# Attention and 2:4-sparse FFN in one kernel: low halves of the FFN weights and of the kept activations moved from GpSimd to VectorE

## The chip, the cores and the metric

One core of a Trainium2 chip runs the whole kernel. The metric is the device time of one launch in microseconds (us), the median of several executions.

## The reference

The input x is 2048 tokens by 512. The result is x plus an attention branch plus a feed-forward branch, both fed by the layer-normalised x:

```python
xn = layernorm(x)
# attention: its own layer norm with gamma, beta; residual is xn
h = layernorm(xn) * gamma + beta
q, k, v = h @ Wq, h @ Wk, h @ Wv
a = softmax(causal(q @ k.T / sqrt(512))) @ v @ Wo + xn
# FFN, 512 -> 2048 -> 512: of each 4 neighbouring hidden values the 2 largest by magnitude stay
g = silu(xn @ Wgate) * (xn @ Wup)
f = keep_top2_of_4(g) @ Wdown
out = x + a + f
```

## The kernel before

Everything is float32. A matrix product is made of three products in the format fp32r: each operand is split into a high half (a rounded copy, made by ScalarE) and a low half (operand minus high half, made by VectorE or GpSimd), and TensorE adds high*high, high*low and low*high. So each product needs one copy and one subtraction per operand ahead of it.

**Three stages.** The preamble (to some 50 us) folds the attention weights. The attention stage (to 387 us) goes over 16 query tiles of 128 tokens. The FFN stage (from 387 us) goes over 16 blocks (`N_Q`); block n makes gate and up by a seven-product block scheme (X_hi, X_lo against `wset`), and ends with the down product of block n - 2 (`down`, L735 to L737).

**The attention stage is driven by one hand-written list, `steps`.** Every engine walks the same list and does its own part of each step, in that order, so a wait in one step holds all later steps of that engine. In tile i the list has: `head i` (turn the first two groups of probabilities, PE; copy them to `pT_hi`, ACT L762; subtract to `pT_lo`, DVE L944), `scores i+1` (PE; DVE L1063 to L1075 takes them out of PSUM and finds the row maximum), the steps of `beside[i]`, and `attend i` (PE L533 to L535; from group 2 on, the turn, copy and subtraction of a group come here; ScalarE's exponentials of tile i + 1 too; DVE L1086 and L1099 write the rows). `between[i]` stands between `head i` and `scores i+1`, `before[i]` ahead of `head i`. PE may write the scores of tile i + 1 before it attends tile i. A group is up to four key tiles; `pT_hi` and `pT_lo` have two slots.

**Chunks.** The 2048 tokens are four chunks of 512. For each chunk c the list also has `stat` and `x_stats` (means and variances, DVE L992, L996), `x_rstd` (GpSimd L493 to L499), `x_scale` (DVE L1002 to L1009), `row_turn` (PE L565, DVE L1037), `row_store` and `row_spread` (ACT-issued DMAs that bring the row statistics back over 128 partitions, L829), `xt_load`, `xh_pre` (DVE L1022, L1024), `xh` (ACT L794, L798 and DVE L1040), `xn` (DVE L1029, L1031), `xn_store` (ACT-issued DMA L837), and the products `z` and `v` (PE, ACT L807, DVE L1049).

**Weight units.** The FFN weights are split during the attention stage, in 40 units: 32 of gate/up (0 to 31) and 8 of down (32 to 39). Unit u is loaded by SP (256 KB, L389; 512 KB for a down unit, L387), GpSimd makes the four sums of the block scheme in it (L508 to L513, gate/up units only), ScalarE makes the high half (L815, L812), GpSimd the low half (L521, L518), and SP stores both halves to DRAM (L400, L401, L396, L397). FFN blocks load them back (`load_set`, L410). The function `paced` strews `unit` steps over the list in proportion to the PE products between the two `RUN` marks of a run. At step `unit n` of a run with lag l: SP stores unit n-l-1 and loads unit n+1, GpSimd makes the sums of n and the low half of n-l, ScalarE makes the high half of n-l. Run 0 has units 0 to 19 (tiles 0 to 7, lag 2, five buffers), run 1 units 20 to 25 (tiles 7 and 8), run 2 units 26 to 39 (tiles 11 to 14, four buffers at 128 to 160 KB). `load_set(0)` waits until all units are stored.

**FFN block n on DVE:** `first_beats` (of block n-2), `add_sum` x2, `last_beats`, `hidden`, `count_beats`, `keep` 0 and 1, `add_sum` x2, `keep` 2 and 3 (all L1152), `hidden` (L1111), the product L1186, `last_block`, `add_down` x4 (L1121). GpSimd makes the four low halves `hs_lo` of the kept activations of block n-2 (L526), for all but the last two blocks, where DVE does it (`kept_lo`, L1210). PE's `down` waits for them by `hs_ready`.

Of the kernel before, what the change touches and what calls it, by code (L numbers as in the profile page):

```python
# [11 lines left out]
P = 128  # L12
# [14 lines left out]
def attention_ffn(nc, x, x_t, qkv_t, o_proj, gamma, beta, w_units, w_down, out):  # L27
# [27 lines left out]
    def fills(kind, n):  # L55
# [22 lines left out]
               7: [("RUN", 0, 1), ("RUN", 1, 0)],  # L78
               11: [*z[3], *v[3], ("RUN", 2, 0)]}
    beside = {0: [xh_pre[1][0], exp[1], v[0][3], xh_pre[1][1]],  # L80
              1: [exp[2], *xh[1]],
              2: [exp[3], x_scale[2], row_turn[2], row_store[2]],
              3: [v[1][2], exp[4], *stat[3], x_stats[3], x_rstd[3], *xn[1], xt_load[2], xn_store[1], row_spread[2]],
# [4 lines left out]
              8: [xn_store[2], v[2][0], v[2][1], ("RUN", 1, 1)],  # L88
              9: [row_spread[3], xt_load[3], v[2][2], *xh_pre[3]],
              10: [v[2][3], *xh[3], *xn[3], xn_store[3]],  # L90
              NT - 2: [("RUN", 2, 1)]}
# [19 lines left out]
    last_chunk = [(24, 28), (56, 60), (88, 92), (120, 124)]  # L111
# [4 lines left out]
    for r, (first, last, _, places) in enumerate(RUNS):  # L116
# [14 lines left out]
    def paced(some, r):  # L131

        first, last, lag, _ = RUNS[r]
# [36 lines left out]
    with ExitStack() as ctx:  # L170
# [33 lines left out]
        def stages(name, part, shape, dt):  # L204
            return [[at(f"{name}{r}_{i}", place[part] * KB, shape, dt) for i, place in enumerate(run[3])] for r, run in enumerate(RUNS)]

        u_hi, u_lo, u_raw = stages("u_hi", 0, [P, NOP, P], F32R), stages("u_lo", 1, [P, NOP, P], F32R), stages("u_raw", 1, [P, NOP, P], F32)
        d_hi, d_lo, d_raw = stages("d_hi", 0, [P, 2, D], F32R), stages("d_lo", 1, [P, 2, D], F32R), stages("d_raw", 1, [P, 2, D], F32)
# [78 lines left out]
        last_hs_ready = sem("last_hs_ready")  # L287
# [71 lines left out]
        def _(sp):  # L359
# [19 lines left out]
            def load_unit(u):  # L379
                s = slot_of[u]  # L380
                if u == RUNS[2][0]:
# [89 lines left out]
        def _(pool):  # L471
# [16 lines left out]
            for kind, n, k in steps:  # L488
# [15 lines left out]
                elif kind == "unit":  # L504
# [9 lines left out]
                    u = n - RUNS[k][2]  # L514
                    if in_run(u, k):
                        pool.wait_ge(unit_hi, u + 1)
                        if is_down(u):
                            nc.gpsimd.tensor_tensor(stage_of(d_lo, u)[:], stage_of(d_raw, u)[:], stage_of(d_hi, u)[:].bitcast(F32),  # L518
                                                    ALU.subtract).then_inc(unit_lo, 1)
                        else:  # L520
                            nc.gpsimd.tensor_tensor(stage_of(u_lo, u)[:], stage_of(u_raw, u)[:], stage_of(u_hi, u)[:].bitcast(F32),  # L521
                                                    ALU.subtract).then_inc(unit_lo, 1)
# [758 lines left out]
```

## Time and profile before

| what | value |
|---|---|
| median of 3 executions | 889.5 us (888.72 to 890.56) |
| the profiled execution's own time | 888.59 us |
| its span, first to last instruction | 886.8 us |
| busy: PE / PE weight load / DVE / ACT / POOL | 820.0 / 668.4 / 549.7 / 308.6 / 255.6 us |
| mean granted TensorE clock | 0.973 of full speed |
| DMA traffic | 167.40 MB, mean 189 GB/s |

PE is TensorE, PEld its weight load, DVE VectorE, ACT ScalarE, POOL GpSimd, SP SyncE. A line number such as L521 is the line of the kernel before. In a timeline the brackets at the end of a row give the idle time of that engine ahead of the instruction and what released it. Names with q (ACTq, SPq) are the instruction queues that issue DMAs. The span has three parts: preamble to about 50 us, attention to 387 us, FFN to the end.

### The profile page before, as it was taken

The numbers are of one execution on the slowest core, as the hardware profiler recorded it, in microseconds if no ns is written. First come the engines' busy times: TensorE is split into PE (matmuls) and PEld (weight loads), VectorE is DVE, ScalarE is ACT, GpSimd is POOL, SyncE is SP. The second block draws the span as 40 slices with busy tenths as digits, with TensorE's granted clock in tenths as the row PEclk, the third lists the DMA queues.
The fourth block names the chain that finished last, engine by engine and source line by source line (L and its number), as shares of the span: only waits on it lengthen the run. The fifth ranks groups of instructions, "written<-read, shape, count | busy, mean of one in ns | idle before, by whom it ended". The sixth has DMA issues, their size and how long they took to land. (4 is left out here: it accounts for less than half of the span.)

```text
span 886.8 us, 9758 instructions
## 1 busy us (share of the span) xinstructions
PE 820.0 (92%) x3635; PEld 668.4 (75%) x3635; DVE 549.7 (62%) x879; ACT 308.6 (35%) x504; POOL 255.6 (29%) x259
## 2 busy tenths in 40 slices
PE   7987963996969999989999999999999999999997
PEld 5775852885758888878788888887788888888875
DVE  6985475352542333373766766779776677768686
ACT  5425325322132334253432423244343324233341
POOL 3154878783000764000022202220220222022110
PEclk9998996998979999999999999999999999999999
DMA  9544797856210589839544336336418633451202
GB/s 323 175 155 154 257 336 263 294 206 239 90 60 12 200 295 368 320 118 406 239 166 166 122 139 248 154 106 275 173 70 295 246 143 119 166 209 53 95 1 95
DMA packets 49600, 167.40 MB, mean 189 GB/s; under 512 B 5088, under 2 KB 5136, under 8 KB 47120
## 3 DMA queue, kind: packets, MB, share of 16 engines
q1 hardware_dynamic: 38912, 144.46, 43.4%
q10 hardware_dynamic: 10640, 22.31, 7.2%
q8 instruction: 29, 0.48, 0.2%
q14 instruction: 19, 0.16, 0.0%
HBM read 116.40 MB, written 50.36 MB: 188 GB/s over the span
## 5 line engine op out<-in xcount | busy, mean ns | idle before, releaser
L657 PE MATMUL bank<-X_hi,wset 128*128 128x512 f32 x448 | 174.7, 390 | 4.9 <-DVE X_lo L958 2.8
L659 PE MATMUL bank<-X_hi,wset 128*128 128x512 f32 x448 | 174.5, 389 | 0.0
L658 PE MATMUL bank<-X_lo,wset 128*128 128x512 f32 x448 | 174.4, 389 | 0.0
L526 POOL TENSOR_TENSOR hs_lo<-hid_a,hs_hi 128x512 fp32r<-128x512 f32 x28 | 41.6, 1517 | 235.4 <-ACT hs_hi L877 235.4
L657 PEld LDWEIGHTS bank<-X_hi,wset 128*128 128x128 f32 x448 | 84.1, 188 | 23.9 <-issue 6.5
L659 PEld LDWEIGHTS bank<-X_hi,wset 128*128 128x128 f32 x448 | 84.1, 188 | 17.5
L658 PEld LDWEIGHTS bank<-X_lo,wset 128*128 128x128 f32 x448 | 84.1, 188 | 17.3
L735 PE MATMUL bank<-dw,hs_hi 128*128 128x512 f32 x224 | 89.2, 398 | 2.2 <-DVE acc L1121 1.2
L526 POOL TENSOR_TENSOR hs_lo<-hid_b,hs_hi 128x512 fp32r<-128x512 f32 x28 | 41.6, 1517 | 170.5 <-ACT hs_hi L877 170.5
L736 PE MATMUL bank<-dw,hs_hi 128*128 128x512 f32 x224 | 87.4, 390 | 0.0
L737 PE MATMUL bank<-dw,hs_lo 128*128 128x512 f32 x224 | 87.4, 390 | 0.0
L1121 DVE TENSOR_TENSOR acc<-bank,acc 128x512 f32<-128x512 f32 x64 | 43.4, 688 | 57.4 <-PE bank L737 57.0
L533 PE MATMUL bank<-v_hi,pT_hi 128*128 128x512 f32 x136 | 58.6, 431 | 16.2 <-DVE pT_lo L944 16.2
L521 POOL TENSOR_TENSOR u_lo<-u_raw,u_hi 128x896 fp32r<-128x896 f32 x32 | 68.0, 2129 | 13.0 <-ACT u_hi L815 13.0
L533 PE MATMUL bank<-xT_hi,zg_hi 128*128 128x512 f32 (+3 forms) x160 | 59.4, 371 | 0.5 <-DVE zg_lo L1049 0.5
L535 PE MATMUL bank<-xT_hi,zg_lo 128*128 128x512 f32 (+3 forms) x160 | 58.3, 365 | 0.0
L534 PE MATMUL bank<-xT_lo,zg_hi 128*128 128x512 f32 (+3 forms) x160 | 58.2, 364 | 0.0
L534 PE MATMUL bank<-v_lo,pT_hi 128*128 128x512 f32 x136 | 56.3, 414 | 0.0
L535 PE MATMUL bank<-v_hi,pT_lo 128*128 128x512 f32 x136 | 56.2, 413 | 0.0
L735 PEld LDWEIGHTS bank<-dw,hs_hi 128*128 128x128 f32 x224 | 42.0, 188 | 18.7 <-DVE acc L1121 7.8
L868 ACT COPY g_sum<-bank 128x512 f32<-128x512 f32 x48 | 27.9, 581 | 68.9 <-PE bank L659 68.9
L815 ACT CAST u_hi<-u_raw 128x896 fp32r<-128x896 f32 x32 | 29.9, 942 | 57.8 <-POOL u_raw L513 52.6
(161 smaller groups left out, 1554.5 us busy)
## 6 DMA issues: line engine op xcount, KB each, us to landing
wset<-w_operands SPq DMA_DIRECT2D x64, 896.0 KB, 8.0
w_operands<-u_hi SPq DMA_DIRECT2D x32, 448.0 KB, 2.5
w_operands<-u_lo SPq DMA_DIRECT2D x32, 448.0 KB, 3.6
dw<-down_operands SPq DMA_DIRECT2D x14, 1024.0 KB, 6.8
u_raw<-w_units SPq DMA_DIRECT2D x32, 256.0 KB, 4.0
xn_t<-xt_raw ACTq DMA_DIRECT2D x8, 512.0 KB, 4.8
d_raw<-L_ffn_w_down SPq DMA_DIRECT2D x8, 512.0 KB, 6.2
down_operands<-d_hi SPq DMA_DIRECT2D x8, 512.0 KB, 5.7
```

What stands on the lines that cost most here:

```text
L521: nc.gpsimd.tensor_tensor(stage_of(u_lo, u)[:], stage_of(u_raw, u)[:], stage_of(u_hi, u)[:].bitcast(F32), ALU.subtract).then_inc(unit_lo, 1)
L526: nc.gpsimd.tensor_tensor(hs_lo_at(d)[r][:], unit_of(down_half[d], r)[:], hs_hi_at(d)[:, r, :].bitcast(F32), ALU.subtract).then_inc(hs_rea ...
L533: pe.matmul(dst, l_hi, r_hi, start=(n == 0 and flags.get("first", True)), stop=False)
L534: pe.matmul(dst, l_hi, r_lo, start=False, stop=False)
L535: last = pe.matmul(dst, l_lo, r_hi, start=False, stop=(n == len(pairs) - 1 and flags.get("last", True)))
L657: pe.matmul(dst[:], u[:, 0, :], x_hi, start=(first and kt == 0), stop=False, skip_group_check=True)
L658: pe.matmul(dst[:], u[:, 0, :], x_lo, start=False, stop=False, skip_group_check=True)
L659: last = pe.matmul(dst[:], u[:, 1, :], x_hi, start=False, stop=(kt == 1), skip_group_check=True)
L735: pe.matmul(dst, s_hi, d_h, start=(r == 0), stop=False)
L736: pe.matmul(dst, s_hi, d_l, start=False, stop=False)
L737: last = pe.matmul(dst, s_lo, d_h, start=False, stop=(r == G - 1))
L1121: nc.vector.tensor_tensor(acc[:, tile, :], down_bank(i, t)[:], acc[:, tile, :], ALU.add).then_inc(added, 1)
```

## The change

- Low halves of the weight units: from POOL (L518, L521) to DVE, as a step of its own, `unit_lo n`, which makes the low half of unit n-1. `paced` now deals out `unit n` and `unit_lo n` in turn.
- ScalarE makes the high half of unit n-1 at `unit n`, SP stores unit n-2 and loads unit n+1 there.
- Two runs in place of three: units 0 to 21 over tiles 0 to 8, units 22 to 39 over tiles 11 to 14; four buffers in both, the one at 180 KB is dropped, and with it DVE's wait in `scores` of tile 8 until it was stored.
- The statistics of the fourth chunk (`stat[3]`, `x_stats[3]`, `x_rstd[3]`) go from tile 3 to tile 1, behind `xh[1]`.
- `row_spread[3]` and `xt_load[3]` are no longer steps of ScalarE in tile 9; SP issues the same DMAs once all units of run 0 are stored (at `unit_lo 23`, in tile 8).
- The low halves of the kept activations of all blocks: from POOL to DVE, two of them ahead of `hidden(n, 2, ...)` and two behind it.

```diff
-    RUNS = ((0, 20, 2, [*last_chunk, (180, 188)]), (20, 26, 1, last_chunk), (26, NU, 1, [(128, 132), (136, 140), (144, 148), (152, 156)]))
-    RINGS = 5
+    RUNS = ((0, 22, (24, 56, 88, 120)), (22, NU, (128, 136, 144, 152)))
+    RINGS = 4
...
-        total, count = sum(passes(step) for step in some), last + lag + 1 - first
+        total, count = sum(passes(step) for step in some), 2 * (last + 2 - first)
...
-                placed.append(("unit", first + done, r))
+                placed.append(("unit_lo" if done % 2 else "unit", first + done // 2, r))
...
+                elif kind == "unit_lo" and n == RUNS[k][1] + 1:
+                    if k == 0:
+                        for s in range(RINGS):
+                            sp.wait_ge(unit_stored[s], 32 * uses_after[k][s])
...
-                    u = n - RUNS[k][2]
-                    if in_run(u, k):
-                        pool.wait_ge(unit_hi, u + 1)
...
-            for d in range(ND - 2):
-                for r in range(G):
-                    pool.wait_ge(hs_hi_ready, G * d + r + 1)
-                    nc.gpsimd.tensor_tensor(hs_lo_at(d)[r][:], unit_of(down_half[d], r)[:], hs_hi_at(d)[:, r, :].bitcast(F32),
-                                            ALU.subtract).then_inc(hs_ready, 1)
...
+                elif kind == "unit_lo" and in_run(n - 1, k):
+                    u = n - 1
+                    hi, lo, raws = (d_hi, d_lo, d_raw) if is_down(u) else (u_hi, u_lo, u_raw)
+                    dve.wait_ge(unit_hi, u + 1)
+                    nc.vector.tensor_tensor(stage_of(lo, u)[:], stage_of(raws, u)[:], stage_of(hi, u)[:].bitcast(F32),
+                                            ALU.subtract).then_inc(unit_lo, 1)
...
                     keep(i, 2)
                     keep(i, 3)
+                    kept_lo(i, 0)
+                    kept_lo(i, 1)
                 hidden(n, 2, 2, g_sum[2], b_tile(n, 1))
+                if picks:
+                    kept_lo(i, 2)
+                    kept_lo(i, 3)
```

The list after the change, where the steps below speak of it (U is `unit`, L is `unit_lo`, AT `attend`, HD `head`, SC `scores`): tile 1 is HD1 SC2 L1 exp2 xh1 stat3 AT1; tile 2 is HD2 SC3 U2 L2 exp3 x_scale2 row_turn2 AT2 U3; tile 5 is HD5 SC6 L11 U12 exp6 xh2 x_scale3 row_turn3 AT5; tile 8 is HD8 SC9 L21 U22 L22 xn_store2 v2.0 U23 v2.1 L23 AT8; tile 12 is HD12 SC13 L27 U28 L28 U29 L29 U30 AT12 L30 U31 L31 U32 L32; tile 13 is HD13 SC14 U33 L33 U34 L34 U35 L35 AT13 U36 L36 U37 L37 U38 L38; tile 14 is HD14 SC15 U39 L39 U40 L40 U41 L41 AT14. Before, tile 12 had SC13 U31 U32 AT12 U33 U34.

## Rows read from the trace of the kernel before

**Rows 1.** The page, part 1: busy time, share of the span and instructions of each engine

```profile
PE 820.0 (92%) x3635; PEld 668.4 (75%) x3635; DVE 549.7 (62%) x879; ACT 308.6 (35%) x504; POOL 255.6 (29%) x259
```

**Rows 2.** Timeline of PE, attention stage (start, duration; in brackets idle time and releaser)

```profile
76.39 0.37 PE L565 MATMUL bank<-ident,row_stat 128*16 128x128 f32 x1 [5.84 <-DVE row_stat L1009]
...
119.74 0.77 PE L533 MATMUL bank<-v_hi,pT_hi 128*128 128x512 f32 x1 [4.46 <-DVE pT_lo L944]
...
147.12 0.37 PE L565 MATMUL bank<-ident,row_stat 128*16 128x128 f32 x1 [15.24 <-DVE row_stat L1009]
...
209.14 0.45 PE L575 MATMUL bank<-ident,raw 128*128 128x128 f32 x1 [6.95 <-issue]
...
261.32 0.79 PE L533 MATMUL bank<-v_hi,pT_hi 128*128 128x512 f32 x1 [7.44 <-DVE pT_lo L944]
```

**Rows 3.** Windows: us; PE, PEld, DVE, ACT, POOL busy; clock, DMA share, GB/s

```profile
209.10:212.50 3.40, 3.36 (x10) 2.78 (x11) 0.54 (x1) 0.00 (x0) 0.00 (x0) 0.60 0.77 306
...
261.30:266.70 5.40, 5.38 (x18) 4.41 (x18) 1.17 (x2) 1.22 (x3) 0.00 (x0) 0.52 0.33 101
```

**Rows 4.** Groups of instructions by line: low halves on POOL and on DVE

```profile
L521 POOL TENSOR_TENSOR u_lo<-u_raw,u_hi 128x896 fp32r<-128x896 f32 x32 | 68.0, 2129 | 13.0 <-ACT u_hi L815 13.0
...
L958 DVE TENSOR_TENSOR X_lo<-X_raw,X_hi 128x1024 fp32r<-128x1024 f32 x14 | 16.2, 1219 | 0.1
```

**Rows 5.** Timeline of DVE, tiles 3 to 5

```profile
106.32 2.46 DVE L992 BATCH_NORM_STATS2 stats<-xw 128x6 f32<-128x512 f32 x4
...
109.11 3.11 DVE L1029 TENSOR_TENSOR xt_raw<-xt_raw,spread 128x1024 f32<-128x1024 f32 x1
...
115.05 1.37 DVE L1031 TENSOR_TENSOR xt_raw<-xt_raw,spread 128x1024 f32<-128x1024 f32 x1
...
126.37 1.23 DVE L1022 TENSOR_TENSOR xh_raw<-xt_raw,spread 128x1024 f32<-128x1024 f32 x1 [4.20 <-DMA spread<-row_stats]
...
142.89 2.34 DVE L1040 TENSOR_TENSOR xT_lo<-xh_raw,xT_hi 128x512 fp32r<-128x512 f32 x1 [0.56 <-ACT xT_hi L798]
```

**Rows 6.** Timeline of ACT and its queue, tiles 3 to 8

```profile
116.92 0.49 ACTq L829 DMA_DIRECT2D spread<-row_stats  x1
...
132.87 0.94 ACT L815 CAST u_hi<-u_raw 128x896 fp32r<-128x896 f32 x1 [6.79 <-POOL u_raw L513]
...
207.73 0.59 ACT L807 CAST v_hi<-bank 128x512 fp32r<-128x512 f32 x1 [3.63 <-DMA xn_t<-xt_raw]
```

**Rows 7.** Timelines of SP, POOL, DVE and PE, tiles 11 and 12

```profile
298.40 0.64 SPq L389 DMA_DIRECT2D u_raw<-w_units  x1
...
302.24 0.46 POOL L508 TENSOR_TENSOR u_raw<-u_raw 128x128 f32<-128x128 f32 x1 [0.73 <-DMA u_raw<-w_units]
...
318.40 0.15 DVE L1075 TENSOR_SCALAR neg_max<-row_max 128x1 f32<-128x1 f32 x1
...
321.21 0.69 DVE L944 TENSOR_TENSOR pT_lo<-bank,pT_hi 128x512 fp32r<-128x512 f32 x1 [2.67 <-ACT pT_hi L762]
...
323.21 0.39 PE L533 MATMUL bank<-v_hi,pT_hi 128*128 128x512 f32 x1
```

**Rows 8.** Set 0 on SP, a window (columns as rows 3), PE's start

```profile
361.64 2.03 SPq L410 DMA_DIRECT2D wset<-w_operands  x4
...
364.00:372.00 8.00, 7.94 (x40) 6.42 (x38) 2.39 (x4) 2.83 (x4) 0.00 (x0) 1.00 1.02 419
...
387.29 0.47 PE L657 MATMUL bank<-X_hi,wset 128*128 128x512 f32 x1 [2.75 <-DVE X_lo L958]
```

**Rows 9.** FFN: DVE in a block, hidden(2), a window (as rows 3), PE near the end

```profile
688.13 3.43 DVE L1152 SCALAR_TENSOR_TENSOR hid_a<-beats_b,hid_a 128x512 f32<-128x512 bf16 x2
...
L1111 DVE TENSOR_TENSOR hid_b<-g_sum,hid_b 128x512 f32<-128x512 f32 x16 | 25.7, 1605 | 17.3 <-ACT g_sum L904 17.1
...
600.00:640.00 40.00, 37.55 (x159) 29.02 (x158) 36.13 (x47) 17.40 (x26) 5.93 (x4) 1.00 0.54 215
...
856.12 0.47 PE L735 MATMUL bank<-dw_last,last_hi 128*128 128x512 f32 x1 [1.47 <-DVE last_lo L1210]
```

More of the change, by code:

```diff
@@ L106, in key_tiles @@
         return [range(g, min(g + TC, i + 1)) for g in range(0, i + 1, TC)]
-    last_chunk = [(24, 28), (56, 60), (88, 92), (120, 124)]
-    RUNS = ((0, 20, 2, [*last_chunk, (180, 188)]), (20, 26, 1, last_chunk), (26, NU, 1, [(128, 132), (136, 140), (144, 148), (152, 156)]))
-    RINGS = 5
+    RUNS = ((0, 22, (24, 56, 88, 120)), (22, NU, (128, 136, 144, 152)))
+    RINGS = 4
     run_of, slot_of, use_of, uses = {}, {}, {}, [0] * RINGS
     uses_after = []
-    for r, (first, last, _, places) in enumerate(RUNS):
+    for r, (first, last, places) in enumerate(RUNS):
         for u in range(first, last):
@@ L131, in paced @@
     def paced(some, r):
-        first, last, lag, _ = RUNS[r]
-        total, count = sum(passes(step) for step in some), last + lag + 1 - first
+        first, last, _ = RUNS[r]
+        total, count = sum(passes(step) for step in some), 2 * (last + 2 - first)
         placed, gone, done = [], 0, 0
@@ L202, in attention_ffn, with stages @@
         spread[2] = spread[1]
[L204 to L208, printed above, removed]
+        def stages(name, inside, shape, dt):
+            return [[at(f"{name}{r}_{i}", (place + inside) * KB, shape, dt) for i, place in enumerate(run[2])] for r, run in enumerate(RUNS)]
+        u_hi, u_lo, u_raw = stages("u_hi", 0, [P, NOP, P], F32R), stages("u_lo", 4, [P, NOP, P], F32R), stages("u_raw", 4, [P, NOP, P], F32)
+        d_hi, d_lo, d_raw = stages("d_hi", 0, [P, 2, D], F32R), stages("d_lo", 4, [P, 2, D], F32R), stages("d_raw", 4, [P, 2, D], F32)
         X_hi = [at(f"X_hi{o}", 8 * o * KB, [P, 2, W], F32R) for o in range(NOP)]
@@ L380, in load_unit @@
                 s = slot_of[u]
[L381 removed]
+                if u == RUNS[1][0]:
                     sp.wait_ge(prod_full, prod_no["z", NCH - 1, KT - 1] + 1)
@@ L418, in _ @@
                 if kind == "unit":
-                    first, last, lag, _ = RUNS[k]
-                    if n == first:
+                    if n == RUNS[k][0]:
                         load_unit(n)
-                    if in_run(n - lag - 1, k):
-                        store_unit(n - lag - 1)
+                    if in_run(n - 2, k):
+                        store_unit(n - 2)
                     if in_run(n + 1, k):
                         load_unit(n + 1)
+                elif kind == "unit_lo" and n == RUNS[k][1] + 1:
+                    if k == 0:
+                        for s in range(RINGS):
+                            sp.wait_ge(unit_stored[s], 32 * uses_after[k][s])
+                        sp.wait_ge(row_stat_stored, 16 * (NCH - 1))
+                        sp.dma_start(spread[NCH - 1][:], row_stats_dram[NCH - 1].rearrange("v t p -> v (t p)").partition_broadcast(P)
+                                     ).then_inc(spread_loaded, 16)
+                        for h in range(2):
+                            sp.dma_start(xt_raw[NCH - 1][h][:], xt_chunks[NCH - 1][:, 2 * h:2 * h + 2, :]).then_inc(xt_loaded[NCH - 1], 16)
             for s in range(RINGS):
@@ L807, in _ @@
                     nc.scalar.copy(dst[:, k, :], prod_bank[no % PROD_RING][:]).then_inc(prod_hi, 1)
-                elif kind == "unit" and in_run(n - RUNS[k][2], k):
-                    u = n - RUNS[k][2]
+                elif kind == "unit" and in_run(n - 1, k):
+                    u = n - 1
                     if is_down(u):
@@ L825, in _ @@
                         act.wait_ge(xn_ready, 2 * n)
-                    if n == NCH - 1:
-                        for s in range(RINGS):
-                            act.wait_ge(unit_stored[s], 32 * uses_after[1][s])
                     act.dma_start(spread[n][:], row_stats_dram[n].rearrange("v t p -> v (t p)").partition_broadcast(P)).then_inc(spread_loaded, 16)
```

35 lines of the change are left out of this document (12 added, 23 removed).

## The prediction

> **What bounds the kernel now.** I read the page's busy shares first: PE works 820.0 of 886.8 us, POOL only 255.6 [rows 1]. So a change on DVE and POOL can only win or lose in the 67 us in which PE stands still, and in the half-speed clock behind such waits. The timeline of PE says where: five long waits of the attention stage, 5.84, 4.46, 15.24, 6.95 and 7.44 us [rows 2], end on work of DVE or ACT. A wait costs more than itself: behind the fourth the granted clock is 0.60 over 3.4 us and behind the fifth 0.52 over 5.4 us [rows 3], so part of that stretch runs at 1.2 instead of 2.4 GHz, which costs 1.4 and 2.6 us more. From 280 us to the end of attention PE waits for almost nothing, and in the FFN it waits only 2.45 us in the window at 600 us and a little near the end [rows 9].
>
> **What is moved, priced.** A unit's low half took POOL 2.13 us for 896 elements [rows 4]. On DVE the nearest row is 1.22 us for 1024 [rows 4], with 0.69 for 512 [rows 7]: between them, 1.09 us. Forty of them add 32 x 1.09 + 8 x 1.22 = 44.6 us to DVE; 56 kept low halves add 56 x 0.69 = 38.6 us. What counts is where they stand in DVE's order.
>
> **A. Tile 2, loss 3.9 us.** PE waits 5.84 us for x_scale2, which DVE reaches right behind xh1, AT1, HD2 and SC3. The change puts the statistics of chunk 3 into this chain (106.32 to 109.11, 2.8 us [rows 5]) and L2 directly before x_scale2 (1.09). Nothing covers them: +3.9. L1 is free, since DVE waits there for ScalarE's first xT_hi. The sums of that time are done long before L2.
>
> **B. Tiles 3 to 5, gain 8.7 us.** The 15.24 us wait ends a chain on DVE, ACT and DMA that starts behind v1.2: statistics, xn1 to 116.42, the row_spread issued at 116.92 which lets DVE go on at 126.37 [rows 5, 6], xh_pre2, AT4, HD5, SC6, ScalarE's xh2, x_scale3. Off it: the statistics (2.8); xn1 takes 7.3 us and would take 4 x 1.22 = 4.9 without POOL's low halves in its way, I take 5.2, so 2.1; on it L7, 1.09. The DMA, 9.45 us from issue to use, begins 3.85 sooner, and I take another 0.9 off because fewer units are in flight (between 0 and 3). Behind it ACT no longer stands 6.79 us for POOL's sums [rows 6], of which I let 1.9 reach the chain (DVE's part of HD5 and the exponentials; between 0 and 6.8); the low half of 2.34 us that met POOL [rows 5] shrinks by 1.6, and of the 1.9 us between its end (145.23) and PE's restart at 147.12 [rows 2] I take 0.5. L9 and L10 lie in DVE's 4.20 us of waiting for the DMA, L11 beside ScalarE. Sum 8.7. The 4.46 us wait goes too but adds nothing: PE would only wait longer at the same place later. If none of the POOL terms were real the gain is 2.8 - 1.1 = 1.7; the most is 12.
>
> **C. Tile 8, gain 7.5 us.** PE's 6.95 us are for v2.0, whose high half ACT makes at 207.73 after 3.63 us of waiting for the xn store [rows 6]; ACT issues that store behind the high halves of six units, each held by POOL. Now only U22, with unit 21, stands ahead of it in tile 8. Unit 21's buffer holds unit 17, made behind SC8. PE stops at 202.19 (209.14 - 6.95); between SC8 and that lie 78 matmuls of 0.236 us (37.55 us for 159 [rows 9]), so SC8 ends at 183.8. DVE's end of it and L18 give 185.7; store, load, sums, copy are 3.84 (a store taken like the load [rows 7]), 3.84, 2.0 and 0.94: 196.3; the xn store with its issue 4.5 and the two halves of v2.0 1.3: 202.1, when PE stops today. Idle 6.95 plus clock 1.4 minus 0.8 left is 7.5. The DMAs of chunk 3, moved to SP, go out when unit 21 is stored, about 205 us, and are wanted only behind SC10 in tile 9: free; if they came late, the wait at 261.32 would grow by what DVE waits. If units run one period late, all 7.5 are lost.
>
> **D. Tile 12, loss 7.5 us.** PE is full here, and before the change nobody in this tile hung on DVE. Now the load of unit 29 is issued at U28 after unit 26 is stored, hence after L27, and L27 comes after SC13, which DVE ends at 318.55 [rows 7]. Then: L27 to 319.6, two stores and the load issued by 320.7, 3.84 from issue to sums (298.40 to 302.24 [rows 7]), sums 2.0, ScalarE's copy 0.94 at U30. Behind it only may ScalarE copy the third group of tile 12 (0.59), and DVE subtract (0.69): 328.8. Today PE begins that group at 323.21 [rows 7]. So 5.5 us idle, and between 1.4 and 2.6 us of clock [rows 3]: I take 7.5. Bounds: 0, if load and sums hide in less than they did; 12, if the load takes twice as long.
>
> **E. Tiles 13 and 14, loss 1 us (0 to 4).** The same chain, with down units: 512 KB to load instead of 256, but no sums, and each tile is 2 us longer on PE. L33 to L35 take 3.7 us (3 x 1.22) in front of DVE's third group, where it idles 2.67 today [rows 7]: 1.0 over.
>
> **F. Set 0, loss 2 us (0 to 5).** The last unit is now made behind SC15, so set 0 goes out some 8 us later than 361.64 [rows 8] and meets the X loads, which ACT issues in head 15. At 419 GB/s [rows 8] set 0 (3.67 MB) takes 8.8 us and X (2.1 MB) 5.0; some 12 us of both after 370 end at 384, with DVE's sums of X still to come, so 2 us of delay on top of today's 2.75 us wait [rows 8].
>
> **G. FFN, gain 3.7 us.** In a block DVE's keep 2 and 3 took 3.43 us with POOL at work [rows 9]; two of 0.69 us at a spacing of 0.6 take 1.29. hidden(2) takes 1.60 there instead of 0.69 [rows 9]. So 2.1 + 0.9 us are freed against 4 low halves at 0.6; two of these lie in DVE's wait for ScalarE's silu: DVE comes out of a block 0.6 to 1.8 us earlier. PE's full blocks don't wait anyway; the 2.45 us at 600 us [rows 9] hang on DVE, and so do the 1.47 us at 856.12 [rows 9]: 2.4 + 1.3. Bounds: 0 and 4.5. DVE's busiest stretch is 36.13 of 40 us [rows 9] and loses work, so no new bound.
>
> **A rule.** The two keeps stretched to 3.43 us [rows 9] stand beside POOL's low halves. The Trainium skill, SBUF — State Buffer, "shared port pair", says DVE with two SBUF inputs and GpSimd take an exclusive lock for the whole instruction. That speaks against part of this change: the sums stay on POOL, and every new low half on DVE has two SBUF inputs, so each could wait one sum. By it E would be up to 1.5 us larger and G as it is.
>
> **Sum.** +3.9 - 8.7 - 7.5 + 7.5 + 1 + 2 - 3.7 = -5.5 us. The profiled execution, 888.59 us (span 886.8), becomes 883.1; the median of the runs is 0.9 above it, so 884.0.
>
> **Rivals.**
> - *No tile 12 stall* (D and E hide, because units run ahead): 884.0 - 8.5 = 875.5. For it: before, ScalarE made its copies there without waiting much. Against: L27 is tied to SC13 by the list. 0.20.
> - *Slower: the DVE-gated load.* The chain of D holds PE in tiles 13 and 14 as well, each at 7.5: 884.0 + 15 - 1 = 898.0. It decides from a load of about 6 us instead of 3.84, which the 419 GB/s of late attention make possible. For it: DVE is freed in bursts, behind SC and AT, and stores and loads then go out together. Against: down units need no sums, which gives back 2 us. 0.15.
> - *Tile 8 keeps its wait* (unit 21 late): 891.5. Against: fewer units per tile. 0.15.
> - *The FFN gives nothing*: 884.0 + 3.7 = 887.7, within the band. For it: PE's waits there are few. 0.10.
> - Forecast: 0.40.
>
> **How the numbers follow.** 0.2% is 1.8 us, about what a measurement of this kernel can tell from no change. Forecast and first rival are faster (0.60); half of the third rival and the second are slower, with the upper edge of the forecast's own unknowns: 0.25; the rest, 0.15, is within. The forecast's own range is 878 to 890; the range reaches to the first rival and nearly to the second: 874 to 896.
>
> **What would show it.** After: the wait at L565 in tile 2 near 9.7 us; the second one near 11 to 14 and ending near 142 us; no long wait in tile 8; a new one near 5.5 us in tile 12 at the third group, with ACT held by POOL's sums; set 0 issued about 10 us behind SC15; keep 2 and 3 at 1.3 us. Wrong if tile 12 shows no wait, if tile 8 keeps one, or if DVE stands for u_hi in tiles 4 to 8.

## The result, and the profile after

| | before | after |
|---|---|---|
| median of 17 executions each, side by side | 889.5 us (887.3 to 891.9) | 892.8 us (890.4 to 898.8) |
| ratio, 95% interval | | 1.0046 [1.0029, 1.0063] |
| span of the profiled execution | 886.8 us | 897.0 us |
| its own time | 888.59 us | 898.84 us |

The change makes the kernel 0.46% slower; forecast were 884.0 us and a gain. The measured 892.8 us lies inside the range of 874 to 896. The profiled execution of after is the slowest of its 17, 6.1 us above their median, so positions in it are some us late; where that matters I compare with other kernels that run the same code there.

Part 1 of the page of the kernel after, the row that answers to [rows 1]:

```profile
PE 823.1 (92%) x3635; PEld 675.6 (75%) x3635; DVE 574.0 (64%) x975; ACT 308.5 (34%) x504; POOL 88.1 (10%) x163
```

POOL has lost 167.5 us of work and DVE gained only 24.3, although 40 + 56 instructions moved to it. Two things hide in that. The groups of the kernel after (busy, mean ns of one, idle before) show low halves cheaper on DVE than on POOL [rows 4], and the work that POOL used to stretch [rows 9] back at its own length:

```profile
L1041 DVE TENSOR_TENSOR u_lo<-u_raw,u_hi 128x896 fp32r<-128x896 f32 x32 | 35.2, 1119 | 2.0 <-ACT u_hi L804 1.9
...
L1146 DVE TENSOR_TENSOR hs_lo<-hid_a,hs_hi 128x512 fp32r<-128x512 f32 x28 | 18.0, 686 | 0.0
...
L1101 DVE TENSOR_TENSOR hid_b<-g_sum,hid_b 128x512 f32<-128x512 f32 x16 | 11.1, 692 | 0.4
...
L1142 DVE SCALAR_TENSOR_TENSOR hid_a<-beats_b,hid_a 128x512 f32<-128x512 bf16 x16 | 10.4, 684 | 0.0
```

Shares of busy time say nothing more. The timeline of PE of the kernel after does (start, duration, in brackets idle time and releaser); it answers to [rows 2] and the last row of [rows 8]:

```profile
80.71 0.37 PE L556 MATMUL bank<-ident,row_stat 128*16 128x128 f32 x1 [9.56 <-DVE row_stat L995]
...
146.93 0.37 PE L556 MATMUL bank<-ident,row_stat 128*16 128x128 f32 x1 [18.46 <-DVE row_stat L995]
...
180.05 0.79 PE L524 MATMUL bank<-xT_hi,zg_hi 128*128 128x512 f32 x1 [3.94 <-DVE zg_lo L1035]
...
209.35 0.30 PE L566 MATMUL bank<-ident,raw 128*128 128x128 f32 x1 [1.01 <-issue]
...
260.27 0.80 PE L524 MATMUL bank<-v_hi,pT_hi 128*128 128x512 f32 x1 [7.43 <-DVE pT_lo L930]
...
327.13 0.80 PE L524 MATMUL bank<-v_hi,pT_hi 128*128 128x512 f32 x1 [5.51 <-DVE pT_lo L930]
...
353.34 0.80 PE L524 MATMUL bank<-v_hi,pT_hi 128*128 128x512 f32 x1 [2.83 <-DVE pT_lo L930]
...
404.81 0.77 PE L648 MATMUL bank<-X_hi,wset 128*128 128x512 f32 x1 [7.05 <-DVE X_lo L944]
...
880.78 0.47 PE L724 MATMUL bank<-dw_last,last_hi 128*128 128x512 f32 x1 [2.72 <-DVE last_lo L1146]
```

Against before, the tile 2 wait grew from 5.84 to 9.56, the two waits of tiles 3 to 5 (4.46 and 15.24) became one of 18.46, the 6.95 of tile 8 shrank to 1.01, and four waits are new or larger: 3.94 in tile 7, 5.51 in tile 12, 2.83 in tile 13 and 7.05 instead of 2.75 ahead of the FFN. The last row answers no row shown of before: there the same wait, for the last block's low halves, is 2.70 us at 871.06, while the 1.47 at 856.12 [rows 9] is gone. Behind each of the new ones PE runs for some us at half speed; behind the one ahead of the FFN the clock is 0.50 from 404 to 408 us, and the rows show the others (windows of the kernel after; us, busy times, granted clock, DMA share, GB/s):

```profile
180.00:184.00 4.00, 3.95 (x9) 3.14 (x10) 1.29 (x3) 1.33 (x2) 1.79 (x4) 0.50 0.98 336
184.00:188.00 4.00, 4.00 (x16) 3.19 (x15) 0.70 (x2) 0.00 (x0) 1.80 (x4) 0.83 0.07 27
...
324.00:328.00 4.00, 0.87 (x2) 0.77 (x3) 0.69 (x1) 3.07 (x4) 2.61 (x6) 0.66 0.99 393
328.00:332.00 4.00, 4.00 (x11) 3.03 (x11) 0.75 (x2) 2.06 (x5) 2.02 (x4) 0.50 0.06 13
352.00:356.00 4.00, 2.66 (x6) 2.15 (x7) 2.16 (x4) 2.40 (x4) 0.00 (x0) 0.58 0.99 349
356.00:360.00 4.00, 4.00 (x12) 3.08 (x11) 0.00 (x0) 1.60 (x2) 0.00 (x0) 0.57 1.03 391
```

A balance from marks that both traces have, after minus before: the row turn of tile 2 +4.3 us; the one of tile 5 -0.2; the matmul behind tile 7's wait +3.7; tile 8's +0.2; tile 9's -1.05 (260.27 against 261.32); the tile 12 matmul at which PE waits now +3.9; head of tile 13 +6.4; of 14 +12.3; of 15 +13.2; start of the FFN +17.5; end of the span +10.2. So everything ahead of the FFN lost 17.5 us, and the FFN gave back 7.3. It gave back 8.5 from its first `down` product on, which stands at +18.7 (464.76 against 446.09).

### The profile page after: what moved, and what is told of

Read it like the earlier page. It is cut to its first block and busy times, and to the rows that moved or that the text cites. A ratio compares the mean times of both kernels' runs of the same rounds, so it can differ in the third digit from the quotient of the medians.

```text
span 897.0 us, 9757 instructions
## 1 busy us (share of the span) xinstructions
PE 823.1 (92%) x3635; PEld 675.6 (75%) x3635; DVE 574.0 (64%) x975; ACT 308.5 (34%) x504; POOL 88.1 (10%) x163
## 5 line engine op out<-in xcount | busy, mean ns | idle before, releaser
L649 PEld LDWEIGHTS bank<-X_lo,wset 128*128 128x128 f32 x448 | 84.8, 189 | 17.5
L724 PE MATMUL bank<-dw,hs_hi 128*128 128x512 f32 x224 | 87.2, 390 | 0.0
L725 PE MATMUL bank<-dw,hs_hi 128*128 128x512 f32 x224 | 87.2, 389 | 0.0
L524 PEld LDWEIGHTS bank<-v_hi,pT_hi 128*128 128x128 f32 x136 | 28.1, 207 | 28.9 <-DVE pT_lo L930 19.7
L1095 DVE TENSOR_TENSOR g_sum<-bank,g_sum 128x512 f32<-128x512 f32 x48 | 33.0, 687 | 26.2 <-ACT g_sum L854 22.3
L726 PEld LDWEIGHTS bank<-dw,hs_lo 128*128 128x128 f32 x224 | 42.0, 188 | 8.7
```

The costliest lines, as they stand in the source:

```text
L524: pe.matmul(dst, l_hi, r_hi, start=(n == 0 and flags.get("first", True)), stop=False)
L649: pe.matmul(dst[:], u[:, 0, :], x_lo, start=False, stop=False, skip_group_check=True)
L724: pe.matmul(dst, s_hi, d_h, start=(r == 0), stop=False)
L725: pe.matmul(dst, s_hi, d_l, start=False, stop=False)
L726: last = pe.matmul(dst, s_lo, d_h, start=False, stop=(r == G - 1))
L1095: nc.vector.tensor_tensor(dst[:], src[:], dst[:], ALU.add).then_inc(summed[m], 1)
```

## The experiments

Each time below is the median against the kernel before on the same chip (its medians were 889.4 to 890.1 us), with the ratio's 95% interval. "After" is 892.8.

**1. Only the kept low halves.** The kernel before with its FFN part changed, nothing else.

```diff
-            for d in range(ND - 2):
-                for r in range(G):
-                    pool.wait_ge(hs_hi_ready, G * d + r + 1)
...
+                    kept_lo(i, 0)
+                    kept_lo(i, 1)
                 hidden(n, 2, 2, g_sum[2], b_tile(n, 1))
+                if picks:
+                    kept_lo(i, 2)
+                    kept_lo(i, 3)
```

> The kernel before with one part of the change alone: the kept low halves of the FFN on VectorE. Theory (the FFN gains, the attention stage loses): the FFN blocks shorten as they did in the change, 0.39 us in each of 14 blocks and some 2 us at the X change, so 889.5 - 8 = 881.5 us. Rival (the FFN gain seen in the one profile is from a later start of the loads and not from this move): 887 to 889 us, block period still 30.30 us.

Measured 880.8 us, 0.9903 [0.9888, 0.9918]. The attention waits are those of before, and from the FFN's first matmul (387.29 before, 388.03 here) to the end of the span it takes 491.1 us instead of 499.5: 8.4 us less. Two windows of the FFN, far from any wait that the prediction named, show where it comes from. The kernel before:

```profile
420.00:450.00 30.00, 28.78 (x128) 23.42 (x127) 22.04 (x31) 12.24 (x22) 5.95 (x4) 1.00 0.57 224
450.00:480.00 30.00, 29.94 (x132) 24.41 (x131) 20.87 (x30) 9.93 (x18) 5.95 (x4) 1.00 0.30 119
```

and this kernel:

```profile
420.00:450.00 30.00, 30.00 (x134) 24.80 (x133) 22.50 (x37) 12.98 (x23) 0.00 (x0) 1.00 0.57 222
450.00:480.00 30.00, 30.00 (x134) 24.82 (x133) 20.49 (x34) 10.15 (x18) 0.00 (x0) 1.00 0.32 127
```

PE starts 134 matmuls in 30 us instead of 128 and 132. In every block before, two weight loads wait a little, which the row of PE's matmuls hides (timeline of the weight loads of the kernel before, one block):

```profile
694.02 0.19 PEld L735 LDWEIGHTS bank<-dw,hs_hi 128*128 128x128 f32 x1 [0.17 <-POOL hs_lo L526]
...
697.76 0.19 PEld L735 LDWEIGHTS bank<-dw,hs_hi 128*128 128x128 f32 x1 [0.47 <-DVE acc L1121]
```

Neither is there in this kernel nor in the kernel after, and a block's period at full clock went from 30.30 to 29.91 us. Which of the two waits is worth how much of the 0.39 us was not separated. Only the second window above shows this alone; in the first, 1.22 us are a plain wait, which run 2 lacks too, so that it isn't due to the low halves (timeline of PE of the kernel before):

```profile
426.92 0.47 PE L657 MATMUL bank<-X_hi,wset 128*128 128x512 f32 x1 [1.22 <-issue]
```

**2. After without that part.** The four `kept_lo` calls out, POOL's loop back in.

> The changed kernel with the kept low halves back on GpSimd. Theory: the weight unit part alone costs 892.8 + 8 = 901 us, block period 30.30 us. Rival (FFN gain not from this move): 893 to 895 us, block period 29.91 us.

Measured 902.8 us, 1.0155 [1.0134, 1.0175], so the part is worth 10.0 us here and 8.6 us in run 1. From the FFN's first matmul to the end: 500.6 us. Both waits of the weight loads are back in each block, and the period is 30.30 us again.

**3. After with the units' low halves on POOL**, executed at the places that the list gives them.

```diff
-                    dve.wait_ge(unit_hi, u + 1)
-                    nc.vector.tensor_tensor(stage_of(lo, u)[:], stage_of(raws, u)[:], stage_of(hi, u)[:].bitcast(F32),
+                    pool.wait_ge(unit_hi, u + 1)
+                    nc.gpsimd.tensor_tensor(stage_of(lo, u)[:], stage_of(raws, u)[:], stage_of(hi, u)[:].bitcast(F32),
```

> The changed kernel with the same list of steps, but the low halves of the weight units made by GpSimd in their steps. Tied loads (SP's load of unit n+1 stands behind a store that stands behind DVE's low half, and DVE makes it only behind scores or attend): GpSimd is not held by scores, so the waits of PE in tile 12 (5.5 us) and tile 13 (2.8 us) go or shrink below 2 us, attention ends about 10 us sooner: 883 to 887 us. Rival (the spacing of the steps and the four buffers are the cause, not the engine): the waits of tiles 12 and 13 stay, 892 us or more.

Measured 878.1 us, 0.9875 [0.9862, 0.9889], beyond what was expected. The DVE low halves cost 14.6 us, more than the whole change loses. In tile 7 ScalarE no longer stands between the copies of z; the wait of 3.94 us is 0.53; tile 8 has no wait; tiles 12 and 13 have 1.97 and 2.49. The wait at the start of the FFN is not better but worse, 8.14 instead of 7.05.

**4. After with SP's load ahead of its store.**

```diff
-                    if in_run(n - 2, k):
-                        store_unit(n - 2)
                     if in_run(n + 1, k):
                         load_unit(n + 1)
+                    if in_run(n - 2, k):
+                        store_unit(n - 2)
```

> The changed kernel with two SP actions of a unit step exchanged: the load of unit n+1 is issued ahead of the store of unit n-2. Tied loads: the load of unit 29 no longer hangs on L27, the wait in tile 12 and the 3.9 us wait in tile 7 go, and the time falls by 8 to 12 us to 881 to 885 us. Rival (DVE's added work itself holds the probabilities): no change in the waits, 892 us. A second rival (DMA bandwidth is full there): waits move to another tile, 889 to 893 us.

Measured 915.0 us, 1.0298 [1.0279, 1.0317]: none of them. Tile 7's wait fell to 1.68 us, but 9.87 stand in tile 13 and 6.80 in tile 14. The load must wait until its buffer's store has *landed*, not only been issued, and now the store of n-2 stands behind that wait. The queue of SP in this kernel shows the chain that results: a load goes out 4.3 us behind the last store of another unit, and the next store only behind that load.

```profile
303.36 0.33 SPq L386 DMA_DIRECT2D u_raw<-w_units  x1
303.74 0.43 SPq L397 DMA_DIRECT2D w_operands<-u_hi  x1
304.21 0.43 SPq L398 DMA_DIRECT2D w_operands<-u_lo  x1
308.55 0.33 SPq L386 DMA_DIRECT2D u_raw<-w_units  x1
```

With four buffers the store of one unit is the condition of another's load, so here holding stores back was worse than holding loads.

**5. DVE in run 0 only** (run 1's low halves on POOL; the edit of run 3 for `k == 1`).

> The kernel after, with the low halves of run 0's units on DVE as there and those of run 1's units (tiles 11 to 14) on POOL, at the same places of the list. Theory (both halves pay): the kernel after is 12 us behind the version with all of them on POOL at tile 8 (260.27 against 248.27 us at the same matmul) and another 9 us by the start of the FFN, in the profiled executions; the medians differ by 14.6, so 14.6 x 9 / 21 = 6.3 us come back here: 886.5 us, with the wait of tile 12 near 2 us instead of 5.5 and tile 13's near 2.5. Rival 1 (only the tail pays, since PE is full there and the waits of run 0 lie beside waits it has anyway): 878 to 880 us. Rival 2 (only DVE's load in run 0 pays, tile 12's wait comes from the 18 units in the tail): 891 to 893 us, tile 12's wait stays above 4 us.

Measured 888.4 us, 0.9982 [0.9972, 0.9993]. 4.3 us come back, less than the theory's 6.3; tile 12's wait is 2.11, tile 13's 2.75, the FFN's start 7.72. So neither rival, and the larger part sits in run 0.

**6. DVE in run 1 only**, the mirror image.

> The kernel after, with run 0's low halves on POOL and run 1's on DVE, the mirror image of a_run0_dve. Theory (the two halves of the cost add up: run 1's is the 4.3 us that its move to POOL gave back, run 0's the other 10.3): 878.1 + 4.3 = 882.4 us (881 to 884), with waits near 5 and 2.5 us in tiles 12 and 13. Rival (they hang together: tail's wait depends on when run 0 ends or on what the clock does): 886 us or more, or 880 or less.

Measured 885.2 us, 0.9941 [0.9925, 0.9957], between theory and rival: 7.6 us come back from 892.8. Alone, run 0's share is 10.3 us (888.4 - 878.1) and run 1's 7.0 (885.2 - 878.1); together they cost 14.6, so 2.7 overlap.

Where run 0's share comes from: ScalarE and POOL in tile 7 of the kernel after. SP issued the load in question at 163.20, behind two stores that waited for DVE's low half behind the scores (timelines of DVE, SP, POOL, then ScalarE and DVE):

```profile
161.01 2.58 DVE L1041 TENSOR_TENSOR u_lo<-u_raw,u_hi 128x896 fp32r<-128x896 f32 x2
...
162.72 0.43 SPq L398 DMA_DIRECT2D w_operands<-u_lo  x1
163.20 0.63 SPq L386 DMA_DIRECT2D u_raw<-w_units  x1
...
170.66 0.46 POOL L513 TENSOR_TENSOR u_raw<-u_raw 128x128 f32<-128x128 f32 x1 [8.01 <-DMA u_raw<-w_units]
...
172.64 0.94 ACT L804 CAST u_hi<-u_raw 128x896 fp32r<-128x896 f32 x1 [4.95 <-POOL u_raw L518]
...
174.10 0.69 DVE L1035 TENSOR_TENSOR zg_lo<-bank,zg_hi 128x512 fp32r<-128x512 f32 x1 [5.68 <-ACT zg_hi L796]
```

7.5 us from the issue to the first sum; ScalarE stands for it with the copy of z behind it, and PE for z. In run 3 ScalarE makes its four copies of z without such a wait, and the same matmul starts at 171.73 instead of 180.05, after 0.53 us.

**7. Statistics back in tile 3.**

```diff
-              1: [exp[2], *xh[1], *stat[3], x_stats[3], x_rstd[3]],
+              1: [exp[2], *xh[1]],
...
-              3: [v[1][2], exp[4], *xn[1], xt_load[2], xn_store[1], row_spread[2]],
+              3: [v[1][2], exp[4], *stat[3], x_stats[3], x_rstd[3], *xn[1], xt_load[2], xn_store[1], row_spread[2]],
```

> The kernel after, with stat[3], x_stats[3] and x_rstd[3] back in tile 3. Theory (the move takes 2.8 us from one wait and gives them to another, and the start of the row DMA decides nothing): tile 2's wait falls from 9.56 to about 6.8 us, the wait ahead of row_turn3 grows from 18.46 to about 21 us, time 892 to 893.5 us. Rival 1 (the prediction's step B: the move gains more in tiles 3 to 5 than it costs in tile 2): 895 to 897 us. Rival 2 (the move costs, because in tile 2 nothing covers it and in tile 3 DVE waits for the DMA anyway): 889.5 to 890.5 us, row_turn3's wait not over 19 us.

Measured 888.7 us, 0.9997 [0.9979, 1.0014]: the move alone costs 4.0 us (rival 2). The timeline of PE:

```profile
76.85 0.37 PE L556 MATMUL bank<-ident,row_stat 128*16 128x128 f32 x1 [6.93 <-DVE row_stat L995]
...
142.56 0.37 PE L556 MATMUL bank<-ident,row_stat 128*16 128x128 f32 x1 [15.01 <-DVE row_stat L995]
```

The first is 3.9 us earlier than in after, the second 4.4, with the statistics in its chain again. What tile 3's chain gains by their absence (2.8 us) it had lost before it began: PE stood 2.6 us longer in tile 2, then restarted at the half clock, and the products of tile 3 reached DVE 4.7 us later (its first low half of z at 89.56 against 84.84).

**8. Statistics back, POOL at the low halves.** Runs 3 and 7 together.

> The kernel after, with the units' low halves on POOL and the fourth chunk's statistics back in tile 3: what is left of the change is the two runs, the chunk 3 DMAs on SP and the kept low halves on DVE. Theory (statistics in tile 1 cost 4.0 us by the run that puts them back, whoever makes the low halves): 878.1 - 4 = 874 us (873 to 875.5), tile 2's wait near 5.8 us instead of 8.28. Rival (with POOL at the low halves tile 3's chain is longer, as in the kernel before, and the statistics there cost what they cost in tile 2): 877 to 879 us.

Measured 879.2 us, 0.9877 [0.9858, 0.9896] (this kernel is `lp_stat3` in later expectations); the rival: no gain over run 3 (878.1). With POOL at the low halves the place of the statistics decides nothing measurable. That also prices the two runs with the chunk 3 DMAs on SP: this kernel differs from run 1 by those and the new places of the steps alone, 879.2 against 880.8, a gain of 1.6 us, which is within the two intervals.

**9. Split 26 and 14.**

```diff
-    RUNS = ((0, 22, (24, 56, 88, 120)), (22, NU, (128, 136, 144, 152)))
+    RUNS = ((0, 26, (24, 56, 88, 120)), (26, NU, (128, 136, 144, 152)))
```

> The kernel after, with the units split 26 and 14 between the two runs instead of 22 and 18. Theory (tail's waits come from the rate: in tile 12 each unit's load, sums, copy and low half, about 12 us with the latencies measured, has less than that between two steps; with 14 units there are 1.25 times as many us between them): waits of tiles 12 and 13 fall from 5.51 and 2.83 to under 3 and 1 us, run 0 loses 2 to 4 us to four more low halves; 888 to 891 us. Rival 1 (a tile's wait is one chain tied to its SC step, whatever the number of units): tile 12's wait 5 us or more, time 893 to 897 us. Rival 2 (run 0 cannot take 26 units): a wait over 5 us in tile 8, 896 us or more.

Measured 892.9 us, 1.0036 [1.0023, 1.0049]. Tile 12's wait is gone, as the theory has it, but 4.00 us stand in tile 13 and 6.47 in tile 8 (rival 2's sign, at less cost than it gave). With DVE at the low halves 22 and 26 units in run 0 come out alike; what is gained in tile 12 is lost in tile 8. A split between the two was not tried with DVE.

**10. Loads issued by POOL**, behind the sums of unit n, so that they pass SP's queue.

```diff
+                    if in_run(n + 1, k):
+                        load_unit(n + 1)
```

> The kernel after, with the loads of units issued by POOL's queue (unit n+1 behind the sums of n, once its buffer is stored) instead of SP's, where each stands behind the store of unit n-2 and so behind DVE's low half of n-2. Theory (the tie of the loads to DVE through SP's queue is the cost): loads go out up to one step sooner, tile 12's wait falls from 5.51 to under 2 us, tile 13's is gone, the 3.94 us wait at 180 too: 880 to 884 us. Rival 1 (the load waits for the store of its buffer, that is unit n-3, and this is what DVE gates; SP's order adds little): 889 to 893 us, tile 12 above 4 us. Rival 2 (a load issued by POOL takes longer to start than one of SP's): 893 to 900 us, with more than 8 us from issue to sums nearly everywhere.

Measured 923.0 us, 1.0372 [1.0357, 1.0386], and no theory's reason. POOL's loads are not slow: 3.65 us in the median of 32 from issue to first sum. But each is issued only when the sums of the unit ahead are done, so POOL stands for each of them in full. Two successive ones of tile 8:

```profile
209.83 0.46 POOL L516 TENSOR_TENSOR u_raw<-u_raw 128x128 f32<-128x128 f32 x1
210.24 0.56 POOL L487 DMA_DIRECT2D u_raw<-w_units  x1
214.75 0.45 POOL L511 TENSOR_TENSOR u_raw<-u_raw 128x128 f32<-128x128 f32 x1 [3.96 <-DMA u_raw<-w_units]
```

So the run swapped one tie for another and says nothing about SP's queue by itself. That DVE's low half holds a load through that queue is shown only by run 12.

**11. X loads ahead of set 0**, both on SP; ScalarE issues no X load.

```diff
+            sp.wait_ge(prod_full, len(prod_no))
...
+            for o, k0, c in ((B11, 0, 0), (T3, 0, 1), (B22, 2, 1), (B21, 2, 0)):
+                load_X(0, o, k0, c)
             load_set(0)
```

> The kernel after, with the four X loads issued by SP directly ahead of set 0 instead of by ACT beside it. Theory (step F's collision: set 0 and the X loads share the DMAs from 385 us and the last X block lands at 401 us, with the sums of X still to come): X lands near 392 us, its sums and halves hide behind set 0, PE then waits for set 0 alone, which lands at about 401: the wait at the start of the FFN falls from 7.05 to 3 to 4 us, time 888.5 to 890 us. Rival 1 (the DMAs share their bandwidth between the transfers whatever the order of issue): the wait stays at 6 to 8 us, 892 to 893.5 us. Rival 2 (the chain of sums and halves of X is the bound, not its loads): the wait stays over 6 us although X lands before 394 us.

Measured 890.3 us, 1.0013 [0.9995, 1.0031]: 2.5 us better than after, 0.3 us outside the theory's range; the two intervals just touch. The wait fell to 4.39 us (theory 3 to 4). The first matmul of the FFN now waits for set 0 (the weights of its first block) itself:

```profile
399.85 0.76 PE L653 MATMUL bank<-X_hi,wset 128*128 128x512 f32 x1 [4.39 <-DMA wset<-w_operands]
```

On top of run 8 the same edit was tried as well.

> As lp_stat3, and the X loads ahead of set 0 on SP. Theory (collision): there both go out at the same time and the wait at the start of the FFN is 8.14 us in the kernel with the low halves on POOL; X first makes it 2 to 4 us, so 4 to 6 us and some of the clock behind it come back: 867 to 871 us. Rival (bandwidth is shared, or PE waits for set 0 as long as for X): within 1 us of lp_stat3.

Measured 877.0 us, 0.9848 [0.9824, 0.9871]: 2.2 us, with the wait at 5.89. Direction as the theory, size about half of it or less, and no more than the intervals allow for chance.

**12. One step moved.** `unit_lo 27` ahead of the scores of tile 13.

```diff
+    steps.remove(("unit_lo", 27, 1))
+    steps.insert(steps.index(("scores", 13, 0)), ("unit_lo", 27, 1))
```

> The kernel after, with one step moved: unit_lo 27 stands ahead of the scores step of tile 13 in the list instead of behind it. Theory (tile 12's wait is one chain that starts with this low half behind the scores: store, load of unit 29 issued at 318.67, sums, ScalarE's copy at 324.93): ScalarE ends the high half of unit 26 at 314.8 us, so DVE can make the low half then and the load goes out near 316.7, 2 us sooner: tile 12's wait falls from 5.5 to 3.5 us, time 890 to 891.5 us. Rival 1 (the units are late all along, the chain is a ring of loads, copies and stores in which this step is not the slow one, and DVE now stands for the high half ahead of the scores): wait 5 us or more, 892 to 895 us. Rival 2 (the step was the only one late): wait under 2 us, 887 to 889 us.

Measured 891.7 us, 1.0022 [1.0010, 1.0034]. The wait, which was forecast at 3.5 us:

```profile
324.93 0.50 PE L527 MATMUL bank<-v_hi,pT_hi 128*128 128x512 f32 x1 [3.59 <-DVE pT_lo L933]
```

So the chain of step D is right: one DVE instruction of 1.07 us behind the scores instead of ahead of them costs PE 1.9 us in this wait. The median is 1.1 us under after's, which the two intervals don't tell from nothing. The load went out at 314.77 instead of 318.67, 3.9 us sooner, but took 8.0 us instead of 6.3 until ScalarE's copy, so half of it was lost again.

**13, 14. The best that came of it.** POOL at the low halves, X first, and the units split 24 and 16, then 26 and 14.

> The kernel after with the units' low halves on POOL, the X loads ahead of set 0 on SP, and the units split 24 and 16. Theory (in the tail the waits of 1.97 and 2.49 us and part of the one before the FFN come from 18 units in three tiles; run 0 has slack while POOL makes the low halves): tile 12's and 13's waits under 1 us each, no wait over 2 us in tile 8, 871 to 875 us. Rival (run 0 has no slack: its end meets the xn store in tile 8 as before): a wait of 3 us or more in tile 8, 876 to 880 us.

Measured 872.8 us, 0.9810 [0.9793, 0.9826], the fastest kernel here, 16.7 us under before and 20.0 under after. Of the waits in tiles 12 and 13 one of 0.97 us is left, and with its last unit stored earlier, set 0 goes out at 363.06 (368.98 with 22 and 18 units, second kernel of run 11) and the FFN starts after 2.81 (timeline of PE):

```profile
337.07 0.50 PE L535 MATMUL bank<-v_hi,pT_hi 128*128 128x512 f32 x1 [0.97 <-DVE pT_lo L931]
...
380.62 0.77 PE L659 MATMUL bank<-X_hi,wset 128*128 128x512 f32 x1 [2.81 <-DVE X_lo L945]
```

What this split gives without X first was not run, so the two aren't priced apart.

> As lp_24_X with 26 and 14 units, the numbers that the kernel before has in its runs. Theory: no wait in tiles 12 and 13, set 0 issued earlier than with 24, and tile 8 begins to wait (0 to 4 us): 871 to 877 us. Rival (tile 8's wait is set by the number of units in run 0, as DVE's version with 26 showed with 6.47 us): 5 us or more there, 877 to 882 us.

Measured 883.0 us, 0.9928 [0.9913, 0.9943]. Two units more, and PE waits 12.07 us for an exponential of ScalarE at 134.68, ahead of tile 5's row turn, and 3.51 in tile 8, where the rival had 5 or more. The wait of 12.07 is in part the old one come sooner: the one ahead of the row turn falls from 16.65 to 9.52, and the row turn stands 5.2 us later than with 24 units (152.25 against 147.06); another 4.3 us are lost up to tile 9. Tiles 12 to 14 have no wait left. Of the two splits tried here, two units decide 10 us.

## Why the prediction was wrong, step by step

The steps that failed are C, E and B. Together they were to gain 15.2 us, and in the profile they lost 1.4. What they had wrong is what hangs on a low half made by DVE, and the time of a load behind it: made by DVE instead of POOL at the same places, the units' low halves cost 14.6 us (run 3). The marks of the balance, taken from step to step in the two profiles:

| step | forecast | measured |
|---|---|---|
| A, to the row turn of tile 2 | +3.9 | +4.3 |
| B, to the row turn of tile 5 | -8.7 | -4.5 |
| C, to the wait of tile 9 | -7.5 | -0.9 |
| D, to the head of tile 13 | +7.5 | +7.4 |
| E, to the head of tile 15 | +1 | +6.8 |
| F, to the start of the FFN | +2 | +4.3 |
| G, the FFN | -3.7 | -7.3 |
| sum | -5.5 | +10.2 |

The medians differ by +3.3 only: the profiled execution of after lies 6.1 us over its median, and where those us stand is not known. Of the three signs under "wrong if" none appeared; of the others, the second wait was 18.46 us and ended at 146.93, instead of 11 to 14 and 142.

**A (+3.9): right, a little low.** Idle 9.56 us against 9.7 forecast; with the restart at the lower clock the row turn stands at +4.3 us, of which 0.4 stood already at 64 us.

**B (-8.7): half.** Between the two row turns 4.5 us were gained. The first part held: the row DMA was forecast to begin 3.85 us sooner against A's shift, and began at 116.37 against 116.92 [rows 6] with the +4.3 in front of it. The rest failed. I took 0.9 us off the DMA's 9.45; it took 11.3 in this profile, 9.6 in run 5 with the same code. And ScalarE did not stop waiting for POOL's sums: 12.07 us in this tile instead of 6.79 [rows 6], because the load in front of the sums was itself late: issued at 119.05, behind a store, it took 11.9 us. The step took the sums' queueing on POOL as the cause; their data was, and in the kernel before already (POOL's first sum, before and after):

```profile
129.83 0.48 POOL L508 TENSOR_TENSOR u_raw<-u_raw 128x128 f32<-128x128 f32 x1 [3.60 <-DMA u_raw<-w_units]
...
130.97 0.61 POOL L513 TENSOR_TENSOR u_raw<-u_raw 128x128 f32<-128x128 f32 x1 [10.96 <-DMA u_raw<-w_units]
```

Run 7 adds what the sum of A and B hid: moving the statistics alone costs 4.0 us.

**C (-7.5): its wait right, its sum wrong.** 1.01 us were left of 6.95 (forecast 0.8). But a new wait of 3.94 us came one tile earlier, with 4 us at clock 0.50 and 4 at 0.83 behind it, 2.0 + 0.7 us more. Together that is 6.6 of the 7.5. The step priced the unit that ends last in tile 8 and none of those before it; the one that held PE in tile 7 was loaded in 7.5 us, not 3.84 (rows at run 6). In run 3, with POOL at the low halves, the same two runs of units leave no such wait.

**D (+7.5): right.** Third group of tile 12, 5.51 us (forecast 5.5), ScalarE held by POOL's sums; clock 0.66 and 0.50 in the two windows that follow. Its load took 4.3 us (3.84 forecast). Runs 5 and 12 confirm the chain.

**E (+1, 0 to 4): too low.** 2.83 us of idle and a clock of 0.58 and 0.57 over 8 us; head 14 lies 5.9 us further behind than head 13, head 15 another 0.9. The step put the down units' loads at nothing ("no sums"); of 512 KB, they took 6.0 to 8.8 us to landing, as long as load and sums of a gate/up unit, and 5.6 to 7.0 in the kernel before. Only a part of E hangs on DVE: with POOL at the tail's low halves the same stretch still loses 4.4 us (run 5), 2.8 (run 3) and 1.3 (run 8); the rest of it comes with the 18 units in three tiles, and is absent with 14 of them in run 14.

**F (+2, 0 to 5): inside its range, its mechanism half right.** The start of the FFN fell back another 4.3 us. Set 0 was issued 384.33 instead of 361.64, a microsecond ahead of the X loads instead of ten:

```profile
384.33 1.96 SPq L407 DMA_DIRECT2D wset<-w_operands  x4
...
385.25 2.51 ACTq L759 DMA_DIRECT2D X_raw<-xn_t  x4
...
400.98 1.99 ACT L769 CAST X_hi<-X_raw 128x1024 fp32r<-128x1024 f32 x2 [3.88 <-DMA X_raw<-xn_t]
```

The last X block was there 15.7 us after the issue (11.1 before). I added both transfers over one bandwidth, which let them end together. X, issued right behind set 0 and not 10 us later, ends late, and all sums of X come behind it. Run 11 shows it. DVE's low halves are not the cause: behind head 15 the start of the FFN falls back as far with POOL at them (4.9, 5.4 and 5.3 us in runs 5, 3 and 8).

**G (-3.7, 0 to 4.5): direction right, size less than half.** 8.4 us by run 1. I wrote "PE's full blocks don't wait anyway"; PE's matmul rows show no wait there, its weight loads do, 0.17 and 0.47 us in each block, and the period shrank by 0.39 us in each of 14 blocks, 5.5 us. So it was also wrong that a change can win only in the 67 us in which PE stands still. The rest are the waits that were forecast: in run 1 some 2.0 us between 597 and 643 us (forecast 2.4) and 1.1 near the end (1.3).

**The error that B, C and E share** is the time of a load: 3.84 us from the issue to the first sum, taken from one row [rows 7], or nothing at all. In after the three loads that held most needed 8.3, 11.9 and 7.5 us in run 0, and the down units' 6.0 to 8.8. The others of run 0 (but for the first four, loaded long ahead) took 3.4 to 6.0 and those of tile 12 3.6 to 5.3 (D's own 4.3), so D came out right. The spread stood in the trace of before, 2.7 to 9.9 us to landing (median 4.0); there ScalarE, POOL and SP ran ahead of DVE, and little of it reached PE. The slower rival (898.0) had this mechanism with 0.15; its condition, a load of about 6 us instead of 3.84, was met by the down units and not by those of tile 12. It asked for 7.5 us in tile 13 and again in tile 14, and measured were about 6 and 1. The result lies between that rival and the forecast.

By runs instead of by steps: kept low halves -8.6; two runs with chunk 3's DMAs on SP -1.6, which the intervals hardly tell from nothing; statistics in tile 1 -1.0, likewise; unit low halves on DVE +14.6; 889.5 becomes 892.9 (measured 892.8). The 14.6 contain the +4.0 of the statistics, which only count with DVE at the low halves.

**The rule of the Trainium skill** (SBUF — State Buffer, "shared port pair"), weighed with up to 1.5 us more for E: DVE's low halves took 1.12 us in the mean against 1.08 for an undisturbed one (the shortest rows), so DVE loses 32 x 0.04 = 1.3 us to it over all units. Single POOL sums beside them stretch from 0.46 to as much as 1.36 us (L515 at 98.61). The trace agrees with the rule in kind, but not with the 1.5 us for E: the eight low halves of down units took 1.22 us each there (1.215 to 1.226), since POOL has no sums for them. The rule explains no part of the loss worth naming.

## What to carry to other kernels

A small instruction that is moved from an idle engine to the busy one costs its place in that engine's order, not its duration: 44.9 us of DVE work cost PE 14.6, because low halves stood behind bursts of scores, and a store, a load, sums and a copy hung on them (followed row by row in tiles 7 and 12). Before such a move, follow what the instruction releases around the whole ring of buffers, and price the load in it by the spread of the trace (here 2.7 to 9.9 us to landing), not by one row. And the two halves of a change should be timed apart: one of them was worth 8.6 us, and the whole looked like a small loss.

## What was not expected of the hardware

- Two weight loads that wait 0.17 and 0.47 us leave no mark in the matmul rows, and still go with 0.39 us in a block of 30: gone together in run 1, back together in run 2.
- A 256 KB load has a median of 3.8 us to landing in after and took up to 11.8; the slowest, issued at 119.05, was under way together with the row DMA of ScalarE's queue (issued at 116.37, 11.2 us to landing). From the issue on POOL's queue to the first sum it took 3.65 us in the median, so the issuing queue made little difference.
- Order of issue matters: with X ahead of set 0 on one queue, all sums of X ran without a wait from 391.8 us, 10.2 us behind the first issue; issued from two queues at nearly the same time, the last X block came after 15.7 us. In time that was 2.5 us, with intervals that just touch.
- Two more units in run 0 (24 to 26) cost 10.2 us with POOL at the low halves, and nothing in the tail was won for it but 1 us of waits.

Left open: why the row DMA took 11.3 us from issue to use in one profile and 9.6 in another of the same code up to it (after, run 5), and how much of the loads' slowness is bandwidth and how much is waiting behind other packets; no run separated these.
